# Layer 0's eight encoder blocks: norms of four streams in one product of column tiles, a new order, all PSUM banks by plan

## The reference

```python
residual = x
q, k, v = x @ Wq + bq, x @ Wk + bk, x @ Wv + bv
Q, K = jax.nn.elu(q) + 1.0, jax.nn.elu(k) + 1.0
KV, Ksum = jnp.einsum('nsh,nsh->nh', K, v), jnp.sum(K, axis=1)
Z = 1.0 / (Q * Ksum[:, None, :] + EPS_Z)
attn = jax.nn.gelu((Q * KV[:, None, :] * Z) @ Wo + bo)
x = _layernorm(attn + residual, ln1_s, ln1_b)
h = jax.nn.gelu(x @ Wf1 + bf1)                     # 128 -> 512
ff = jax.nn.gelu(h @ Wf2 + bf2)                    # 512 -> 128
x = _layernorm(ff + x, ln2_s, ln2_b)

def _layernorm(x, scale, bias):
    m = jnp.mean(x, axis=-1, keepdims=True)
    v = jnp.mean(jnp.square(x - m), axis=-1, keepdims=True)
    return (x - m) * jax.lax.rsqrt(v + EPS_LN) * scale + bias
```

## Time and profile before

| | |
|---|---|
| median of three runs | 1715.57 us (1710.26, 1715.57, 1718.10) |
| profiled execution, first to last instruction (span) | 1711.5 us |
| TensorE, VectorE, ScalarE, GpSimd busy over the span | 1571.5, 1224.6, 1151.8, 262.1 us |
| mean granted TensorE clock | 0.964 of full speed |
| layer 0's branches | 36 to 820 us |

### The profile page before, as it was taken

One profiled execution on the slowest core, in us unless ns is written; L12 is line 12 of the kernel. 1 busy time (PEld: TensorE's weight loads), 2 busy tenths in 40 slices (PEclk: granted clock), 3 DMA queues, 4 the chain that ended last, 5 costly groups with the idle time before them and its releaser, 6 DMA issues. The chain is left out here.

```text
span 1711.5 us, 19967 instructions
## 1 busy us (share of the span) xinstructions
PE 1571.5 (92%) x7054; PEld 682.4 (40%) x7054; DVE 1224.6 (72%) x1736; ACT 1151.8 (67%) x1604; POOL 262.1 (15%) x227
## 2 busy tenths in 40 slices
PE   6999999999999999999799989999877678678998
PEld 3333233333333333332344446665432455333674
DVE  5977777777777777773143325876399889997997
ACT  5688888888888888888333357534475568333663
POOL 1000111111010111111000010000179200582000
PEclk8999999999999999999999988999999889888999
DMA  6200101010010100000252112111353677630000
GB/s 199 57 12 7 25 13 26 13 25 13 7 25 7 25 13 7 13 0 1 60 101 62 37 39 64 46 39 44 99 191 130 204 232 249 177 132 12 1 1 25
DMA packets 66716, 104.18 MB, mean 61 GB/s; under 512 B 9015, under 2 KB 32534, under 8 KB 66596
## 3 DMA queue, kind: packets, MB, share of 16 engines
q1 hardware_dynamic: 55354, 65.15, 14.0%
q10 hardware_dynamic: 9216, 33.56, 6.0%
q0 software_dynamic: 2048, 4.20, 0.8%
HBM read 86.92 MB, written 15.87 MB: 60 GB/s over the span
## 5 line engine op out<-in xcount | busy, mean ns | idle before, releaser
L708 DVE TENSOR_REDUCE best<-quad 128x2 f32<-128x1024 f32 x256 | 309.7, 1221 | 130.5 <-PE quad L498 128.1
L622 ACT ACTIVATE weights<-quad 128x1024 f32<-128x1024 f32 x256 | 255.8, 1029 | 28.6 <-PE quad L523 28.2
L2629 PE MATMUL quad<-l_st,ident 128*128 128x512 f32 x256 | 130.3, 653 | 44.3 <-DVE l_st L2940 44.2
L540 PE MATMUL quad<-weights,values 128*32 128x512 f32 x1024 | 136.4, 605 | 0.4 <-ACT weights L622 0.4
L110 PE MATMUL quad<-q,wf 128*128 128x512 f32 x256 | 121.5, 606 | 0.7 <-DVE q L659 0.3
L110 PE MATMUL quad<-hid,wf 128*128 128x512 f32 x256 | 116.6, 599 | 0.0
L566 ACT ACTIVATE hid<-quad,col 128x512 f32<-128x512 f32 x128 | 84.9, 689 | 21.4 <-PE quad L110 21.2
L734 POOL TENSOR_TENSOR sq_all<-cen_all 128x512 f32<-128x512 f32 x64 | 65.2, 1039 | 213.9 <-DVE cen_all L653 213.9
L110 PE MATMUL quad<-sq_all,mean_w 128*128 128x512 f32 x176 | 94.7, 638 | 1.8 <-ACT sq_all L1367 0.9
L498 PE MATMUL quad<-ks,qs 48*128 48x512 bf16 x512 | 89.5, 385 | 6.8 <-DVE best L708 6.3
L2629 PEld LDWEIGHTS quad<-l_st,ident 128*128 128x128 f32 x256 | 50.7, 209 | 112.3 <-DVE l_st L2940 60.3
(11 more groups left out here) (454 smaller groups left out, 3035.6 us busy)
## 6 DMA issues: line engine op xcount, KB each, us to landing
l_bs<-xd_dram ACTq DMA_DIRECT2D x32, 512.0 KB
l_c_rows<-xd_dram ACTq DMA_DIRECT2D x32, 512.0 KB
end_cs<-comb SPq DMA_DIRECT2D x32, 256.0 KB, 3.9
l_cs<-comb SPq DMA_DIRECT2D x32, 256.0 KB, 3.7
l_weights<-in_F_w SPq DMA_DIRECT2D x30, 257.0 KB, 4.7
wf<-in_L_f SPq DMA_DIRECT2D x16, 256.0 KB, 2.6
l_rows<-in_F_w SPq DMA_DIRECT2D x15, 257.0 KB, 6.0
qs<-q_dram SPq DMA_DIRECT2D x16, 192.0 KB, 3.5
```

What stands on the lines that cost most here:

```text
L540: last = nc.tensor.matmul(out[32 * j:32 * j + 32, :], values[:, kt, GH * g + j, :], weights[p % BUFS][:, j % 2, j // 2, :], start=(kt == 0 ...
L622: nc.scalar.activation(weights[p % BUFS][:, slot, :, :].rearrange("p a t -> p (a t)"), doubles.of("weigh", m, i), ACT.Exp, scale=scale).th ...
L708: nc.vector.tensor_reduce(heads[:, :, slot, qt, c], doubles.of("search", m, i).rearrange("p (a t) -> p a t", a=2), AX.X, ALU.max).then_inc ...
L2629: last = nc.tensor.matmul(y[d][:, c:c + BANK], core.ident[:, :], st[n % RING][:, c:c + BANK], start=False, stop=(s == NS - 1), skip_group_ ...
```

## The change

**Norms.** One group serves all four streams: of block i, either streams 0 and 1 with their first norm and streams 2 and 3 with their second of block i - 1, or streams 0 and 1 with their second and streams 2 and 3 with their first. There are 17 groups (`NORMS`), of which the first and the last have two streams. `means` is four products of `mean_w[:, 0:32]`, one a stream, that write partitions 32s to 32s + 31 of one bank. ScalarE copies that bank to `mq` of two streams (`rows`), GpSimd spreads row 32s over all partitions of `sq[s]` (`partition_broadcast`, one after another, `alone`), VectorE subtracts it from the residual (`centred`), ScalarE squares (`square`), `vars` is again four products of 32 columns, ScalarE takes log and exponential of one bank for four streams, and GpSimd spreads the four rows. `scaled` and `affine` stay.

**Work moved.** The squares go from GpSimd to ScalarE; `divide`, `second_values` and the last sum into x go from GpSimd to VectorE.

**PSUM.** All eight banks are one tensor, and a table (`HELD_0`) names the bank or pair of each product; `Banks` makes each wait for the last tenants of just these. **Order.** `PLAN_0` gives each step of each block and chunk its own place in one order of 0 to 2760. The core of the diff:

```diff
-    bank = [core.quad[b // 4][:, b % 4 * BANK:(b % 4 + 1) * BANK] for b in range(8)]
-    singles = Ring(bank[0:3], [(att(s, i, n), s, (s, i, n)) for s in EVERY for i in range(B) for n in OUTPUTS_ATT.split()] +
...
+class Banks:
+    def __init__(self, buffers, planned):
+        self.buffers, self.place, self.tenants, last = buffers, {}, {}, {}
+        for time, key, held in sorted(planned):
+            self.tenants[key] = list(dict.fromkeys(last[b] for b in held if b in last))
+            self.place[key] = held
+            last.update((b, key) for b in held)
...
+PLAN_0 = {
+    "k": (
+        0, 244, 587, 932, 1277, 1623, 1967, 2309, 9, 255, 598, 943, 1285, 1634, 1978, 2320, 26, 432, 777, 1122, 1467, 1816, 2156, 2499, 75, 427, 772,
+        1117, 1462, 1807, 2151, 2494,),
...
+    def members(p):
+        i = p // 2
+        if p % 2:
+            return [(0, i, "n2"), (1, i, "n2"), (2, i, "n1"), (3, i, "n1")]
+        return [(s, i, "n1") for s in (0, 1) if i < B] + [(s, i - 1, "n2") for s in (2, 3) if i]
...
+        rows = lambda p, row: mq[(2 if p % 2 or p == NORMS - 1 else 0) + row]
...
-                def norm(s, i, pre, src, plan):
-                    yield plan(s, i, pre + "centre")
-                    pe.wait_ge(st.dve_done[s], sdve.value("res" + pre[1], i))
-                    single_free(pe, s, i, pre + "centre")
-                    product(nc, singles.of(s, i, pre + "centre"), [(core.centre_w[:, :], src)]).then_inc(st.pe_done[s], 1)
-                    yield plan(s, i, pre + "var")
-                    pe.wait_ge(st.pool_done[s], spool.value(pre + "square", i))
-                    single_free(pe, s, i, pre + "var")
-                    product(nc, singles.of(s, i, pre + "var"), [(core.mean_w[:, :], st.sq[s])]).then_inc(st.pe_done[s], 1)
+                def norms():
+                    for p in range(NORMS):
+                        yield at("means", p)
+                        for s, i, pre in members(p):
+                            pe.wait_ge(st.dve_done[s], sdve.value("res" + pre[1], i))
+                        bank_free(pe, p, "means")
+                        for s, i, pre in members(p):
+                            last = nc.tensor.matmul(banks.of(p, "means")[32 * s:32 * s + 32, :], core.mean_w[:, 0:32], k[s][:, :], start=True, stop=True)
+                        last.then_inc(means_ready, 1)
...
+                        yield at("copy_means", p)
+                        act.wait_ge(means_ready, p + 1)
+                        nc.scalar.activation(rows(p, 0)[own, :], banks.of(p, "means")[own, :], ACT.Identity).then_inc(mean_copied, 1)
...
+                        yield at("var_log", p)
...
+                        nc.scalar.activation(rows(p, 1)[own, :], banks.of(p, "vars")[own, :], ACT.Ln, bias=core.eps[1e-6][own, :]).then_inc(var_logs, 1)
+                        yield at("rstd", p)
...
+                        nc.scalar.activation(rows(p, 1)[own, :], rows(p, 1)[own, :], ACT.Exp, scale=-0.5).then_inc(rstd_ready, 1)
...
+                    act.wait_ge(st.dve_done[s], sdve.value(pre + "centred", i))
+                    nc.scalar.activation(st.sq[s], st.cen[s], ACT.Square).then_inc(st.act_done[s], 1)
...
-                    nc.vector.tensor_copy(st.cen[s], singles.of(s, i, pre + "centre")).then_inc(done, 1)
+                    dve.wait_ge(pool_done, turns.value(pre + "mean", s, i))
+                    nc.vector.tensor_tensor(st.cen[s], k[s][:, :], st.sq[s], ALU.subtract).then_inc(done, 1)
...
+                        nc.vector.tensor_tensor(heads_of(m), heads_of(m), inv[:, :], ALU.mult).then_inc(heads_done, 1)
...
-                            nc.gpsimd.tensor_tensor(st.sq[s], st.cen[s], st.cen[s], ALU.mult).then_inc(st.pool_done[s], 1)
+                    alone(pre + "mean", s, i)
+                    pool.wait_ge(mean_copied, p + 1)
+                    nc.gpsimd.partition_broadcast(st.sq[s], rows(p, 0)[32 * s:32 * s + 1, :]).then_inc(pool_done, 1)
...
+                    alone(pre + "rstd", s, i)
+                    pool.wait_ge(rstd_ready, p + 1)
+                    nc.gpsimd.partition_broadcast(st.sq[s], rows(p, 1)[32 * s:32 * s + 1, :]).then_inc(pool_done, 1)
```

More of the change, by code:

```diff
@@ new lines, in rows_of, with group_of, held @@
+    def rows_of(p):
+        streams = [s for s, i, pre in members(p)]
+        return slice(32 * streams[0], 32 * streams[-1] + 32)
+    def group_of(s, i, pre):
+        return 2 * i + s // 2 + (pre == "n2")
+    pool_banks = core.banks[:, :].rearrange("p (b n) -> p b n", n=BANK)
+    def held(name, *index):
+        plan, n = HELD_0[name], 0
+        for i, size in zip(index, SIZES_0[name]):
+            n = n * size + i
+        return plan[n]
+    singles = ([(at(n, s, i), (s, i, n), (held(n, s, i),)) for s in EVERY for i in range(B) for n in OUTPUTS_0.split()] +
+               [(at(n, p), (p, n), (held(n, p),)) for p in range(NORMS) for n in ("means", "vars")] +
+               [(at(n, m), (m, n), (held(n, m),)) for m in range(CHUNKS) for n in ("turn", "sums")] +
+               [(at("use", m, 0), (m, "use"), (held("use", m, 0),)) for m in range(CHUNKS)])
@@ L358, in layer_0_branches @@
+    turns = Turns([(at(n, s, i), (n, s, i)) for s in EVERY for i in range(B) for n in SPREADS_0.split()])
     with ExitStack() as ctx:
@@ L754, in _ @@
+                        yield from norm(s, i, "n2")
                 nc.gpsimd.memset(ones[:, :], 1.0).then_inc(ones_set, 1)
```

626 lines of the change are left out of this document (456 added, 170 removed), and 101 rows, old and new, of tables (HELD_0, PLAN_0, PLAN_ATT, PLAN_NET).

## The result

The changed kernel takes 1672.07 us in the median of 4 runs (1670.13 to 1673.88), the kernel before 1715.47 in the same comparison: a ratio of 0.976, 95% interval 0.9734 to 0.9786. 1678 was predicted. Runs more than 1.5% above the fastest of the same kernel are left out of every median and ratio of this document.

A forecast was written before the change was run, and what follows sets the result against it. TensorE bounds before, ScalarE after: 43.5 us a period, 45.3 at 0.96, 2.7 less over sixteen periods is -44; with +6 at the ends, -38, from 1715.57 to 1678 us. Range 1640 to 1738.

The forecast's parts named there:

- The saving by column tiles: TensorE in layer 0: 128 full products removed (124 us), 34 column-tile groups at 1.00 us added, stage sum 681 us.
- tiles in line: TensorE's norm groups: four tiles one after another take 3.9 us and the gain is gone, 1715 or so; within chance 0.08.
- 697 was predicted: ScalarE's sum in layer 0: net +22.3 us, 43.5 a period, passing TensorE's 42.4 to become the bound.
- shared access: VectorE meeting GpSimd's spreads: 0.33 us each, eight make 2.6 a period, 39.3 in all, still under 43.5.
- rival D: Every spread blocks VectorE for its whole length: 46.9 us a period, 1698 us; chance 0.08.
- The efficiency and the ends: Layer 0: leading engine busy 0.96, so 45.3 us a period; first and last norm groups exposed, +6 us.
- Rival B: Layer 0's bound is met to the full: 43.5 us a period, 1643 us; chance 0.12.
- E: ScalarE stays at its old share of 0.877 in layer 0: 49.6 us a period, 1741 us, slower; chance 0.10.
- The loading of the spread's code: One-time GpSimd load in the stage's first microseconds, price unknown, counted in the +6 us.
- the loop through the spreads: Means to next means in layer 0: 29.8 + 8s us for spread s, 40.0 at 1.27, hidden under 43.5.
- The sign that the prediction named for this: In the changed profile: the first spread's waiters as largest idle of all engines would show the loop is the bound.
- rival C: The loop bounds: a spread of 2.56 us makes a turn 50.3, 1752 us, slower, deciding from 2.3; chance 0.14.

The follow-up runs named there:

- e4: Kernel before the change with each of the 64 variance products multiplied twice: 1774.99 us, ratio 1.0338 to the kernel before.
- e7: Changed kernel with stream 0's column tile 128 wide and stream 2's 64, so tiles overlap: 1754.31 us, ratio 1.0213 to the kernel before.
- e11: Changed kernel with the 256 attention exponentials over 768 of their 1024 columns: 1657.74 us, ratio 0.9669 to the kernel before.
- e12: Changed kernel with three of the four products that make ff: 1672.73 us, ratio 0.979 to the kernel before.
- e5: Changed kernel with each of the 128 spreads done twice: 1785.76 us, ratio 1.0378 to the kernel before.
- e6: Changed kernel with each of the 128 spreads done three times: 1912.02 us, ratio 1.1138 to the kernel before.
- e9: Changed kernel without the 64 spreads of means: 1672.12 us, ratio 0.9751 to the kernel before.
- e10: Changed kernel with ScalarE's copy, log and exponential of a norm group right behind their products in the order: 1742.26 us, ratio 1.0158 to the kernel before.
- e8: Changed kernel with its 64 squares on VectorE instead of ScalarE: 1737.57 us, ratio 1.0129 to the kernel before.

## Why the prediction was right, and where it was not

**What bounds the kernel before.** TensorE, as predicted: e4.

**TensorE.** The saving by column tiles is as priced, 1.00 us a group, and e7 shows that it needs their running side by side. (In the prediction's case of tiles in line each tile has two records, as many as a full product, and not half; the 3.9 follows from that and was met.) The sum of the stage was 681 and is 692.64, 43.0 a period instead of 42.4. The rise was not split further.

**ScalarE.** 697 was predicted, 685.97 measured. That it catches up with TensorE is right (43.0 against 43.0); that it passes it by 1.1 us is not, and e11 and e12 do not settle which leads. Most of the 11 us too many lie in rows that the change leaves alone: the 256 exponentials are busy 249.2 us instead of 255.8 and the 128 of `hid` 80.3 instead of 84.9, while the squares came out dearer (0.664 in the mean, not 0.596). The number of table loads is as counted (48 and 47 in the whole span), at 1.283 us.

**VectorE.** 585 was predicted, 605 measured. The term is shared access, which the prediction had described (0.33 a meeting) and then left out of the stage's sum: 64 scale steps at 0.13 more than 0.69, 64 centre steps at 0.09 and 64 affine steps at 0.11 make 21 us. By the rows nothing is held up for a whole spread, so rival D is there in kind and not in size. The Trainium skill, SBUF — State Buffer, Who interferes with whom, has exclusive access of the one that comes first. The trace agrees in who is late, in the tensor_scalar steps too (0.53 outside, 0.91 in a spread), and not in how much: the second one loses 0.38 of 0.67 us overlapped, or 0.50 of 0.63, and not the whole overlap. Here the measurement decides.

**The efficiency and the ends.** 0.96 of the leading engine gave 45.3; measured are 45.60, and 94% to 95% for both. e11 and e12 show that this level stays when either is relieved. Rival B (the bound met in full) stood at 1643 and E (ScalarE at its old share of 0.877) at 1741; neither came. No row gave the 0.96: it was chosen between 1.00 and 0.948, and that it fits is in part luck, since what e5 shows to be paid is a loop that it does not contain. The ends cost 2 us instead of 6. So in layer 0 -44 + 6 = -38 was forecast and -39 + 2 = -37 came, two misses of 5 and 4 us that nearly cancel; most of what is left of the 41.6 between the spans is layer 1's. The loading of the spread's code, which the prediction put into the +6 without a price, leaves no visible mark: the first spread, at 54.22 us, starts when ScalarE's copy is there.

**The step that failed is the loop through the spreads.** The prediction said: 29.8 + 8s, 40.0 at 1.27, hidden to 1.7. At the measured spread, 0.96 in the mean, the formula gives 37.5. A turn is 46.2 us in the timeline above, with a shorter spread than I took. I had added up the durations of one chain, with the network half alone, as if each of its steps could start when its input is there. They can't: each stands in its engine's fixed order behind attention's work (the copy 2.5 us after its product). From the end of the second spreads (331.99) to the next group of means (360.32) the turn takes 28.3 us, where I had 21.6 for the network half and 1.2 for scale and affine. In this turn it is not even the network half that is last: its residual is ready at 356.19 and that of the attention half, which the formula leaves out, at 359.67. In the turn before, the network half was last (L1108, TensorE waits 0.51). So slack is not turn against period: it is what each step in the queue has by itself. e5 and e6 show that there is hardly any upward, about 1 us a period by the table above. e9 shows that by shortening the spreads of means there is nothing to win. The sign that the prediction named for this, the waiters of the first spread as the largest idle of all engines, did not fire: VectorE waits 11.2 us for spreads of means in 137 to 682 and 39.2 for products of the search. Only e5 found it.

**Two errors that cancelled.** The spread was priced at 1.27 and takes 1.02 and 0.91 in the mean: 128 x 0.31 = 39 us less. At the slope of e5 a spread of 1.27 would have cost up to these 39 us, and the time would have been near 1710: worked out, not run. So the forecast of 1678 stood on a slack that doesn't exist, and it was luck that the spread was shorter than its price. In rival C a spread of 2.3 us was to eat the whole gain; by the measured slope 0.34 us more on each of the 128 spreads (43.4 / 128) does it, some 1.3 us.

**Layer 1.** The 4 us there were not foreseen. They go with a higher granted clock at its start. Why it is higher was not tested.

**Left open.** How the gain divides between the norms in column tiles, the bank plan and the new order: undoing the banks alone was not tried. Which of ScalarE and TensorE leads in the changed kernel, and whether these two or the order of waits through the norm pass set its period, is not settled. Whether fewer spreads of `rstd` would pay is not known either.

## What to carry to other kernels

Where engines run in a fixed order, do not price a chain by adding up its steps and comparing with the period: read for each step how long it stands between its input and its start, for that is all its slack, and expect to pay nearly all that goes beyond it. A latency that fits can be removed at no gain, and a wait that looks idle may be cover for the neighbours (e9, e10). Four narrow products beside each other are worth it when they replace full ones on the bounding engine, but count at once what the other engines have then: here ScalarE came up to TensorE, and of 5.6 us a period that TensorE was to save, 2.4 came. Look at the granted clock of such an experiment before its price is read: every variant here that makes the engines wait (e5, e6, e8, e10) also shows a lower one.

## What the runs showed of the hardware

A spread of one row over 128x512 f32 takes 0.80 us alone or beside VectorE's maxima, which read PSUM, and up to 1.34 where it meets a VectorE step between SBUF tensors. The one that starts second pays: VectorE with 1.07 instead of 0.69 and 0.91 instead of 0.53, the spread with 1.30 instead of 0.80. Four column tiles of 32 take 1.00 us together, and 3.99 when two of them are made wide enough to overlap the others (e7). The granted clock over the steady part is 1.00 in the changed kernel, 0.97 in e8, 0.96 in e5 and e10 and 0.90 in e6, where TensorE waits more between its products; so a part of what these four cost may be the clock and not the loop.
